# Layer norms centred by a matmul, biases folded into the next weights, and projections in array tiles

## What is computed

```python
# block 1, per token over 64 channels
x_ln = layernorm(x, ln1_w, ln1_b)
q, k, v = split(qkv_w @ x_ln)                       # 4 heads of 16
x = x + proj_w @ softmax(q k^T / 4) v + proj_b      # 1024 x 1024 scores per head
x = x + fc2_w @ gelu(fc1_w @ layernorm(x, ln2_w, ln2_b) + fc1_b) + fc2_b
# block 2
t = t + window_attention(norm(t))                   # 8 heads of 64, window of 32 tokens
t = t + rnn(batchnorm(W @ norm(t)))                 # sigmoid recurrence over the tokens
```

## Time and profile before

| | us |
|---|---|
| runs of the kernel | 541.43, 546.31, 546.99; median 546.31 |
| profiled execution | 541.36 |
| its span | 539.4, so 2.0 lie around it |
| busy: TensorE, VectorE, ScalarE | 461.1, 328.0, 291.6 |
| mean granted clock of TensorE | 0.963 of 2.4 GHz |

### The profile page before, as it was taken

The page is one execution under the profiler, slowest core; times in us unless marked ns, Lnnn a source line. Parts: engine busy times, 40 slices in busy tenths (PEclk is TensorE's granted clock), DMA queues, the critical chain, the costliest instruction groups (busy, mean ns, idle before and its releaser), DMA issues.

```text
span 539.4 us, 7934 instructions
## 1 busy us (share of the span) xinstructions
PE 461.1 (85%) x3257; PEld 178.3 (33%) x3257; DVE 328.0 (61%) x605; ACT 291.6 (54%) x499; POOL 12.9 (2%) x15
## 2 busy tenths in 40 slices
PE   7886889988989798787998987889998879995884
PEld 2442322222234332232233322222243323542583
DVE  3696868789748653689568654696332644514414
ACT  3442665755674365564873574648855655172242
POOL 9000000000000000000000000000000000000000
PEclk9896998989999999999999999999999998997897
DMA  8100180006300000017000000000000000000003
GB/s 295 28 1 2 41 136 1 1 1 121 56 2 1 1 1 1 1 33 144 0 2 1 1 1 2 0 0 1 2 2 1 1 0 1 2 1 1 1 1 79
DMA packets 6196, 13.09 MB, mean 24 GB/s; under 512 B 1296, under 2 KB 3600, under 8 KB 6032
## 3 DMA queue, kind: packets, MB, share of 16 engines
q1 hardware_dynamic: 6160, 12.58, 10.4%
HBM read 9.07 MB, written 3.41 MB: 23 GB/s over the span
## 4 chain that ended last, share of the span: by engine, by line
PE 66%; DVE 21%; ACT 8%; issue 3%; DMA 1%; SPq 1%; DVEq 0%; ACTq 0%
DVE part_max L1156 8%; PE O L725 8%; PE R L773 5%; PE T L690 4%; PE T L710 4%; PE R L621 3%; PE R L710 3%; PE R L882 3%; PE R L629 3%; PE R L690 3%; PE R L843 3%; PE R L870 2%; PE T L600 2%; PE R L857 2%; DVE zs L1267 2%
## 5 line engine op out<-in xcount | busy, mean ns | idle before, releaser
L1156 DVE TENSOR_REDUCE part_max<-T 128x1 f32<-128x512 f32 x170 | 112.0, 682 | 29.5 <-PE T L690 29.4
L1016 ACT ACTIVATE probs<-T 128x512 f32<-128x512 f32 x150 | 85.9, 597 | 41.2 <-PE T L710 41.0
L1016 ACT ACTIVATE probs<-R 128x512 f32<-128x512 f32 x106 | 62.0, 597 | 57.9 <-PE R L710 57.6
L690 PE MATMUL T<-KX,QX 96*128 96x512 bf16 x170 | 63.6, 395 | 9.7 <-DVE part_max L1156 8.3
L725 PE MATMUL O<-probs,VT 128*32 128x512 f32 x512 | 68.6, 611 | 1.1 <-ACT probs L1016 1.1
L1156 DVE TENSOR_REDUCE part_max<-R 128x1 f32<-128x512 f32 x86 | 57.4, 681 | 11.8 <-PE R L690 11.7
L710 PE MATMUL T<-QX,KX 99*128 99x512 bf16 x150 | 54.7, 389 | 7.5 <-DMA QX<-mx_part 5.5
L710 PE MATMUL R<-QX,KX 99*128 99x512 bf16 x106 | 40.3, 389 | 1.4 <-ACT probs L1016 0.7
L690 PE MATMUL R<-KX,QX 96*128 96x512 bf16 x86 | 33.2, 394 | 2.7 <-DVE part_max L1156 2.4
L773 PE MATMUL R<-xp,abd 128*128 128x512 f32 x64 | 32.3, 603 | 2.7 <-DVE xp L1125 2.6
L1040 ACT ACTIVATE p<-R 128x1024 f32<-128x1024 f32 x14 | 14.3, 1023 | 31.6 <-PE R L843 31.6
(11 more groups left out here) (220 smaller groups left out, 648.1 us busy)
## 6 DMA issues: line engine op xcount, KB each, us to landing
qk_scratch<-qk_part SPq DMA_DIRECT2D x6, 384.0 KB, 4.4
zs<-early SPq DMA_DIRECT2D x1, 2048.0 KB, 7.8
QX<-qk_scratch SPq DMA_DIRECT2D x3, 384.0 KB, 4.9
KX<-qk_scratch SPq DMA_DIRECT2D x3, 384.0 KB, 7.0
result<-probs SPq DMA_DIRECT2D x2, 512.0 KB, 5.1
s_rest<-rest SPq DMA_DIRECT2D x1, 882.0 KB, 10.1
X<-x SPq DMA_DIRECT2D x2, 384.0 KB, 11.9
QX<-qk_scratch SPq DMA_DIRECT2D x3, 256.0 KB, 7.7
```

Source lines behind the costliest of these rows:

```text
L690: mm(ring["max_piece", b, half, i], QX[b % 2][0:KQ, half, h, nt * P:(nt + 1) * P], KX[b % 2][0:KQ, kh, h, :], start=True, stop=True).then_ ...
L1016: A(probs[:, u % 2, h, :], ring["scores", b, u, h], ACT.Exp, scale=HD ** -0.5).then_inc(g["exp_done"], 1)
L1156: nc.vector.tensor_reduce(part_max[:, row, kh:kh + 1], ring["max_piece", b, half, i], AX_X, ALU.max).then_inc(g["max_red"], 1)
```

## The change

- **Centring by a matmul.** L621 multiplies by `center`, the identity less the means, so the bank holds the centred values. The subtraction on VectorE goes; ScalarE squares from PSUM, and `ln_scale` reads PSUM. The bank stays in use until then.
- **Weights in the multiplication, biases through the weights.** Norms 1 and 2 end in one operation, (centred x weight) x rstd. The bias of norm 1 is multiplied by the query and key weights on chip (four matmuls of one column, two copies) and is added where the parts are split; its part in the values goes through `wv` and the output projection into `proj_bias`; norm 2's goes through fc1 into `fc1_bias` (three matmuls of one column and three small operations on ScalarE, at `products`).
- **Tiles.** Queries and keys become four matmuls of 64 x 64, each in its own quarter of the array; half 0 of both goes to one bank and half 1 to the other. fc1's two matmuls use 64 rows each.
- **Relayout.** Bank and parts now hold a half each, not queries or keys, so the writes to DRAM are four of 3 parts, not two of 6. The six products are the same in another order: eight reads, not six.
- `center` (64 KB) joins the first load and `wproj_c` the later one. The ring takes R's banks back a few items later, at batch 2's norm 1.

The diff, cut:

```diff
@@ -20,12 +20,12 @@
 PARTS = 3
 
 
-RUNS = (((0, 2), (1, 1), (2, 0)), ((0, 1), (1, 0)), ((0, 0),))
+RUNS = (((0, 0), (1, 1)), ((0, 1), (0, 2)), ((1, 0), (2, 0)))
 TERMS = sum(len(r) for r in RUNS)
 KQ = TERMS * HD
 
 
-PART_OF_ROW = (sum((tuple(q for q, _ in r) for r in RUNS), ()), sum((tuple(PARTS - 1 - k for _, k in r) for r in RUNS), ()))
+PART_OF_ROW = tuple(sum((tuple(term[q] for term in r) for r in RUNS), ()) for q in range(2))
...
@@ -409,9 +417,11 @@
 
         def ln_dst(b, which, i=0):
 
+            if which < 3:
+                return x_ln[:, :]
             if which == 3:
                 return xn
-            return ln_bufs(b, which, i)["ln_d"] if which < 3 or (b, which) == (B - 2, 4) else xh[:, ln_cols(b, which, i)]
+            return ln_bufs(b, which, i)["ln_d"] if (b, which) == (B - 2, 4) else xh[:, ln_cols(b, which, i)]
 
         def pair(b):
             return T[:, 0:2, :] if apart(b) else R[:, 0:2, :]
...
@@ -458,8 +469,9 @@
                     shared = range(len(banks))
                     owner[4] = owner[5] = "qk_rst", 4
                     owner[6] = "v_copied", 2
-                elif item == ("scores", 1, 0, 0):
+                elif item == ("ln_mean", 2, 1, 0):
                     shared = (*OWN, *LENT)
+                    norm_free.extend((owner[4], owner[5]))
                 elif name == "blk_scores" and rest == [0]:
                     shared, lent_free[b] = OWN, [owner[i] for i in LENT]
                 elif name == "blk_den" and rest == [STAGES - 1]:
@@ -529,20 +541,23 @@
                     return
                 sp.wait_ge(g["qk_lo"], b + 1)
                 for half in range(2):
-                    sp.dma_start(scratch[b, half].rearrange("q r d h n -> (d h) (q r) n"),
-                                 qk_rows[half_rows(half), :, :]).then_inc(g["qk_dram"], 16)
-                sp.wait_ge(g["qk_dram"], 32 * b)
+                    for q in range(2):
+                        sp.dma_start(scratch[b, half, q].rearrange("r d h n -> (d h) r n"),
+                                     qk_part[qk_rows(q, half), half, :, :]).then_inc(g["qk_dram"], 16)
+                sp.wait_ge(g["qk_dram"], 64 * b)
                 if b >= 2:
                     sp.wait_ge(g["st_mm"], H0 * UNITS * (b - 1))
                 row = 0
                 for run_ in RUNS:
-                    rows = len(run_) * HD
                     for q, dst in enumerate((QX[b % 2], KX[b % 2])):
-                        p0 = run_[0][0] if q == 0 else PARTS - 1 - run_[0][1]
-                        sp.dma_start(dst[row:row + rows, :, :, :].rearrange("p a h n -> p a (h n)"),
-                                     scratch[b, :, q, p0:p0 + len(run_)].rearrange("a r d h n -> (r d) a (h n)")
-                                     ).then_inc(g["qk_in"], 16)
-                    row += rows
+                        parts = sorted({term[q] for term in run_})
+                        p0, n = parts[0], len(parts)
+                        for again in range(len(run_) // n):
+                            at = row + again * HD
+                            sp.dma_start(dst[at:at + n * HD, :, :, :].rearrange("p a h n -> p a (h n)"),
+                                         scratch[b, :, q, p0:p0 + n].rearrange("a r d h n -> (r d) a (h n)")
+                                         ).then_inc(g["qk_in"], 16)
+                    row += len(run_) * HD
 
             def shift_rows(b, half):
 
...
-                        pe.wait_ge(g["mx_r"], 3)
+                        pe.wait_ge(g["fold_done"], 3)
+                    elif b == 2:
+                        for free in norm_free:
+                            pe.wait_ge(g[free[0]], free[1])
                 elif which == 2:
                     pe.wait_ge(g["x1_done"], b + 1)
                 elif which == 3:
                     pe.wait_ge(g["x2_done"], b + 1)
                 elif which == 4:
                     pe.wait_ge(g["x3_done"], b + 1 + i)
-                mm(ln_bank(b, which, i, 0), t["mean_c"], ln_in(b, which, i), start=True, stop=True).then_inc(g["ln_mean"], 1)
+                mm(ln_bank(b, which, i, 0), t["center"], ln_in(b, which, i), start=True, stop=True).then_inc(g["ln_ctr"], 1)
 
             def ln_var(b, which, i):
...
                     keep_clock(8)
-                pe.wait_ge(g["ln_out"], affine.index([b, 1, 0]) + 1)
-                mm(R[:, 0, :], t["wq"], x_ln[:], start=True, stop=True).then_inc(g["qk_mm"], 1)
-                mm(R[:, 1, :], t["wk"], x_ln[:], start=True, stop=True).then_inc(g["qk_mm"], 1)
+                    for half in range(2):
+                        for q, w in enumerate(("wq", "wk")):
+                            last = mm(bias_bank(half)[qk_rows(q, half), 0:1], t[w][half_rows(half), half_rows(half)], v["ln1_b"][half_rows(half), :],
+                                      start=True, stop=True)
+                        last.then_inc(g["bias_mm"], 1)
+                pe.wait_ge(g["ln_norm"], ln_no(b, 1) + 1)
+                for half in range(2):
+                    for q, w in enumerate(("wq", "wk")):
+                        last = mm(R[qk_rows(q, half), half, :], t[w][half_rows(half), half_rows(half)], x_ln[half_rows(half), :],
+                                  start=True, stop=True)
+                    last.then_inc(g["qk_mm"], 1)
 
             def project_v(b):
...
 
             def fc1(b):
 
-                pe.wait_ge(g["ln_out"], affine.index([b, 2, 0]) + 1)
-                for half in range(2):
-                    last = mm(pair(b)[:, half, :], t["wfc1"][:, half, :], x_ln[:], start=True, stop=True)
+                pe.wait_ge(g["ln_norm"], ln_no(b, 2) + 1)
+                for half in range(2):
...
@@ -892,10 +914,13 @@
                 mm(wx_bank(b, i), t["w_in"], ln_dst(b, 4, i), start=True, stop=True).then_inc(g["wx_mm"], 1)
 
             def products():
+
                 pe.wait_ge(g["early_in"], 16)
                 pe.wait_ge(g["rest_in"], 16)
                 pe.wait_ge(g["pool_fills"], 8)
                 pe.wait_ge(g["lay_in"], LAID)
+                mm(R[:, 1, 0:1], t["wv"], v["ln1_b"], start=True, stop=True)
+                mm(R[:, 1, 1:2], t["wfc1"][0:C, 0, :], v["ln2_b"][0:C, :], start=True, stop=True).then_inc(g["fold_mm"], 1)
 
                 for h in range(H1):
                     for half in range(2):
@@ -907,6 +932,8 @@
                         last = mm(O[half_rows(half), h * C:(h + 1) * C],
                                   t["w1v"][:, h, :], t["w1u"][:, h, :], start=True, stop=True)
                 last.then_inc(g["gbd_mm"], 1)
+                pe.wait_ge(g["fold_done"], 2)
+                mm(R[:, 1, 2:3], t["wproj_c"], v_bias[:], start=True, stop=True).then_inc(g["fold_mm"], 1)
 
             pe.wait_ge(g["fills"], 1)
             keep_clock(7)
...
                 elif b:
-                    act.wait_ge(g["qk_dram"], 32 * (b - 1))
-                for q in range(2):
-                    act.wait_ge(g["qk_mm"], 2 * b + q + 1)
-                    A(hi_rows[:, q, :], R[:, q, :], ACT.Copy).then_inc(g["qk_hi"], 1)
+                    act.wait_ge(g["qk_dram"], 64 * (b - 1))
+                else:
+                    act.wait_ge(g["bias_done"], 2)
+                for half in range(2):
+                    act.wait_ge(g["qk_mm"], 2 * b + half + 1)
+                    A(hi_rows[:, half, :], R[:, half, :], ACT.Identity, bias=qk_bias[:, half:half + 1]).then_inc(g["qk_hi"], 1)
...
@@ -1111,37 +1145,38 @@
                     nc.vector.tensor_copy(m1_part[M1_ROWS:M1_ROWS + UQ, gs, :], t["unit_tokens"][M1_ROWS:M1_ROWS + UQ, :])
                 nc.vector.tensor_copy(unit_sel[:], t["unit_select"]).then_inc(g["unit_sel_done"], 1)
 
-            def ln_mean(b, which, i):
-                if which == 1 and b == 1:
-                    dve.wait_ge(g["x_in"], 32)
-                dve.wait_ge(g["ln_mean"], ln_no(b, which, i) + 1)
-                TT(ln_bufs(b, which, i)["ln_d"], ln_in(b, which, i), ln_bank(b, which, i, 0), ALU.subtract).then_inc(g["ln_ctr"], 1)
-
             def ln_scale(b, which, i):
                 buf = ln_bufs(b, which, i)
                 dve.wait_ge(g["ln_rstd"], ln_no(b, which, i) + 1)
                 if which == 3 and b:
                     dve.wait_ge(g["s1_mm"], STAGES * b)
-                TT(ln_dst(b, which, i), buf["ln_d"], buf["ln_r"], ALU.mult).then_inc(g["ln_norm"], 1)
+                dst, centered = ln_dst(b, which, i), ln_bank(b, which, i, 0)
                 if which < 3:
-                    dve.wait_ge(g["ln_norm"], ln_no(b, which, i) + 1)
-                    TS(x_ln[:], ln_dst(b, which), v[f"ln{which}_w"], v[f"ln{which}_b"], ALU.mult, ALU.add).then_inc(g["ln_out"], 1)
+                    last = STT(dst, centered, v[f"ln{which}_w"], buf["ln_r"], ALU.mult, ALU.mult)
+                else:
+                    last = TT(dst, centered, buf["ln_r"], ALU.mult)
+                last.then_inc(g["ln_norm"], 1)
 
             def project(b):
                 if b:
```

(27 more changed lines are left out.)

50 lines of the change are left out of this document (30 added, 20 removed).

## The result

The changed kernel took 540.29 us as the median of 20 runs (532.76 to 542.49), the kernel before 546.37 us beside it (20 runs, 540.58 to 552.07): a ratio of 0.9895, with a 95% interval of 0.986 to 0.993. A second set of six runs gave 539.34 us and 0.9883 (0.983 to 0.9936).

The account below looks back on a forecast made before the run. TensorE's stream, elsewhere a chain of dependent operations, was taken as the bound, with VectorE close behind. Terms summed to -13.4 on the chain; between 9.9 and 13.4 it took 11, so 546.31 - 11 = 535.3 us, range 528 to 543.5.

Parts of the forecast that it names:

- Start (-2.8): From the start to the first relayout: the parts end near 17.3 and not 20.16, 2.8 us sooner.
- The 1.9 for x_ln: At the start: the new scaling operation does not wait for GpSimd's fill, so x_ln is ready near 12.0, not 13.9.
- Tiles of the projections: Query and key projections: four tiles overlap, 1.98 us becomes 1.08 plus 0.1 for the handover, worth 0.8 each.
- Tiles of fc1: fc1's matmuls: two tiles of 64 rows overlap, worth 0.8 each, between bounds of 0 and 0.8.
- The term of 4.8 for six places: Two projections and four fc1 in tiles at 0.8 each: 4.8 us less on the chain.
- Norms in the attention (-4.45): Norms 1 and 2 inside the attention: three subtractions (2 x 0.7 + 0.55) and five merged operations at 0.5 leave the chain.
- The split of its maxima: Batch 2: without the subtraction between its steps on VectorE, scores wait less for the row; -1.1, taken at -0.9.
- Products (+0.4): At about 37 us, around the 64 products: three added one-column matmuls on TensorE's chain cost 0.4 us.
- relayout (+0.3, -0.45): First relayout through DRAM: extra reads and writes cost 0.3; batch 1's last part comes 0.45 earlier by norm and tiles.
- Tail (-0.7): Norm 4 of batch 3: bare subtraction of the first part goes, -0.6; paired norms at 446 us, -0.1.
- the granted clock falls where it did not: Rival, chance 0.06: TensorE idles more at projections and fc1; each half-rate stretch costs up to 2 us, eight give 551.
- the first rival: Chance 0.12: start and tail gain, but in the attention ScalarE's exponentials or a bank of R take it back; 542 us.

Follow-up runs that it names:

- The full-array run: Queries and keys projected on the whole array instead of four tiles, against the changed kernel; 533.35 us, 0.9803 of the kernel before.
- the two experiments: Against the changed kernel: second VectorE instruction of norms 1 and 2 back, 542.72 us; subtraction back in all 17 norms, 538.35 us.

## Why the prediction came out as it did

**Start (-2.8): 2.9 measured, one third of it by luck.** The 1.9 for x_ln was right in mechanism and size. The selector hid the subtraction's going (Square starts at 7.92 behind it), the new form took 0.75 and did not wait, and putting a tensor_scalar back cost the forecast 1.9. The other 0.9 was given to the tiles and came from the granted clock.

**Tiles of the projections: the step failed.** I priced them at the rows of the two matmuls in the chain, 1.98 for 1.08. But ScalarE's first rounding needs only the first matmul and takes 0.6 to 0.7, as long as the second one nearly; that the second stood in the chain said that it was last by a hair, not that 0.8 us lay bare. The full-array run shows 0.04 to 0.1. The start's number was right all the same because a second error cancelled this one. For the stretch at 0.50 the prediction counted nothing, taking what runs there for the V projection mostly; but the second query and key matmul ran there too, for 1.91 us where it takes 0.86. With x_ln at 12.0 this stretch is gone, and about 1.0 us of chain with it: 3.01 from the projection to the second rounding before, 2.02 on the full array in the new kernel (12.01 to 14.03), 1.77 with tiles.

**Tiles of fc1: the step failed in three of four places.** The overlap was right (bound of 0.8, 1.13 us for four records). What I did not look at was Gelu's own predecessor on ScalarE: exponentials and 1.28 us of table load, hidden until then under fc1. Only the last batch gained, 0.85. The term of 4.8 for six places was mis-sized: 0.85 to 0.95 remains on the chain, and all tiles together show as 0.7 ± 0.9 at equal clock.

**Norms in the attention (-4.45): sizes right, count too high.** Norm 2 of batches 0 and 1 gained 1.06 each from its first matmul to fc1 (forecast 1.2: the subtraction is worth 0.61, not 0.7, the second instruction 0.44, not 0.5). But only 0.68 of it reached Gelu, behind the same exponentials and load; the second instruction's part is gone there. Norm 1 of batch 3 gained 0.56, and norm 1 of batch 2 has 0.52 and 0.59 by the two experiments (0.5 and 0.55 forecast). **Norm 2 of batch 2 gained next to nothing**: 0.15 from the first matmul to fc1, where 0.5 was forecast, and 0.8 for the tiles. The split of its maxima is 1.1 us shorter as forecast (1.31 for 2.41 us from its first step to its DMA), but TensorE had waited only 0.38 us for the row that it makes. The lead (by how much sooner the changed kernel reaches a step than the kernel before) grows by 0.3 us over that stretch, for the 0.9 forecast. The chain of the changed kernel in front of fc1 says why the norm is worth so little there:

```profile
358.82 0.23 PE T L712
...
359.08 1.30 DVE part_max L1191 x2
...
360.42 0.39 PE R L712
360.81 1.00 PE O L747 x8
361.81 0.34 PE R L732
...
362.23 1.09 ACT probs L1045 x2
...
363.33 1.28 ACT L1057
```

x_ln has been ready since 361.02, but TensorE has values and scores written ahead of fc1 and ScalarE has exponentials: VectorE's part of the norm is not on the chain at all. I had carried batches 0 and 1 over to it.

**Products (+0.4) and relayout (+0.3, -0.45): the sum right, the parts not quite.** The lead falls from 2.90 at the first maxima to 2.20 behind the products (37.17 for 39.37), so the three matmuls cost 0.7. It is 2.44 at 43.8 us, because two matmuls of the maxima ran at half rate before and take 0.43 for 0.68. Up to the relayout it grows to 2.71 (-0.27), and the relayout costs nothing: the row of maxima lands 3.34 us after its issue for 3.48. The lead is 2.85 behind it (2.55 forecast).

**Tail (-0.7) and the clock.** The tail's subtraction was worth the 0.6: the step from the first part's centring matmul to Square fell from 2.27 us to 1.39, and 0.3 of that is the matmul's own. The clock took more. The lead was 6.6 us at 454 us and 3.6 at 469. The twelve matmuls on unused data ahead of the window rows, which are there to keep the clock up, ran in the new lower stretch and took 5.2 us for 2.7. VectorE's copy that the next matmul reads had ended 3.9 us before that matmul started; in the kernel before it was 1.4. At 498.5 us the lead was 4.5, and behind the longer last stretch, at 511.5, it was 2.8. That is the mechanism of the rival "the granted clock falls where it did not", which had 0.06 and a price of 2 us for each stretch. It came about in part: 3.6 us in the two profiled executions (0.70 x (25.2 - 20.0)), between 0 and 1.5 us in the mean, and the 551 us never. That every place of a tile would cost a stretch was wrong; but the place was worth a look, since the kernels with fewer tiles lost 19 to 21 us of clock for the changed one's 27, which is 4 to 6 us of time.

**The sum.** Of 13.4 on the chain 7.2 came at equal clock. Of the missing 6.2, about 3.9 are the tiles', 1.0 what norm 2 of batches 0 and 1 does not bring to Gelu (1.36 of 2.4), and 1.0 norm 2 and the split of batch 2. The start's 1.0 us of clock stands outside this account, so it closes only to about 1 us. I had cut to 11 because VectorE would stand close behind. It was right that something did; it was ScalarE and TensorE's written order more than VectorE. The time fell inside the range (528 to 543.5), and between the forecast's 535.3 and the first rival's 542, on the latter's side. That rival had the truer mechanism: it gave the attention's gain to other waits, ScalarE's exponentials first, but put all of it at nothing, where some 3 us stayed. So the range held by its width; the forecast's largest term, the tiles, failed.

What stays open is why the kernels with either set of tiles taken out keep the higher clock. They lose fewer stretches in the last 100 us, but a run with only the projections' tiles out has no reason of its own to differ there. And taking fc1's tiles out is not enough: the run with Identity and fc1 on the full array has the changed kernel's stretches (438 to 442, 458 to 466, 489 to 504 us). That filling the tail's waits keeps the clock up there is shown by the kernels that do so.

## What to carry over

Before a shorter operation is counted, ask what the next one waits for besides it: the first half of the result, a table load, or its own engine's queue; a row in the chain shows that it was last, not by how much. Where a term comes out right, check that its parts did, too: here a clock counted at nothing paid for tiles worth nothing. In a kernel whose TensorE clock varies, compare at equal clock and list the lost clock beside it, since a part can be neutral in work and cost 1% in clock. Once an edit shortens TensorE's work ahead of waits, look at the waits behind it first; with the tiles in, filling them was worth as much here as all the norms' subtractions (4 and 3 us).

## What the runs showed of the hardware

- Two fp32 tiles of 64 rows x 128 columns on the two row halves take 1.13 us together and one alone 1.12, where two full matmuls take 1.99. The overlap is lost when matmuls over 112 rows stand between the two: with four of them there, the second tile started 2.03 us after the first.
- An ACT_TABLE_LOAD cost 1.28 us and started 0.02 us after the activation ahead of it.
- A query and key matmul of 0.86 us on the chain took 1.91 where the granted clock was 0.50.
- One us of lost clock cost 0.70 us of time in this kernel (0.60 with the longest executions left out), and the changed kernel lost between 20 and 32 us of clock from one execution to the next.
